# Projections: both rotary products on VectorE in a row, the low parts of queries and keys both on GpSimd

## What is computed

```python
q = (x @ Wq.T).reshape(B, T, 2 * H, hd)          # 16 half heads of 8
k = (x @ Wk.T).reshape(B, T, 2 * H, hd)
q = apply_rotary(rmsnorm(q), cos, sin)
k = apply_rotary(rmsnorm(k), cos, sin)
# apply_rotary: concatenate([x1 * c + x2 * s, -x1 * s + x2 * c])
```

## Time and profile before

| | us |
|---|---|
| median of 3 runs | 825.85 (824.96 to 826.49) |
| the profiled execution | 824.34 |
| its span in the profile | 822.6 |
| of it, from the first to the last sum L328 of the project phase | 23.25 to 108.83 |
| VectorE busy in the whole span | 589.5 |

### The profile page before, as it was taken

One profiled execution on the slowest core, in us unless ns is written; L12 is line 12 of the kernel. 1 busy time (PEld: TensorE's weight loads), 2 busy tenths in 40 slices (PEclk: granted clock), 3 DMA queues, 4 the chain that ended last, 5 costly groups with the idle time before them and its releaser, 6 DMA issues. The chain is left out here.

```text
span 822.6 us, 14081 instructions
## 1 busy us (share of the span) xinstructions
PE 629.0 (76%) x4241; PEld 324.2 (39%) x4242; DVE 589.5 (72%) x1424; ACT 480.6 (58%) x828; POOL 356.2 (43%) x506
## 2 busy tenths in 40 slices
PE   1366555999999999999999728877759877998920
PEld 1244332333333333333333216656536544654510
DVE  3899996779797979797977676797625443586734
ACT  2356665899999999999999512223324333444430
POOL 0234353234343434344433211117635777666653
PEclk9776865999999999999999956868759999999965
DMA  4200005940000000000000040012112222334241
GB/s 120 75 14 26 26 1 109 153 94 27 26 25 25 25 25 25 25 25 25 25 27 2 1 154 26 26 32 72 51 50 71 74 77 64 107 89 127 67 134 51
DMA packets 52978, 45.31 MB, mean 55 GB/s; under 512 B 5936, under 2 KB 47216, under 8 KB 52688
## 3 DMA queue, kind: packets, MB, share of 16 engines
q1 hardware_dynamic: 45600, 34.97, 16.5%
q0 software_dynamic: 4544, 9.35, 3.3%
q10 hardware_dynamic: 2800, 0.58, 0.3%
HBM read 15.72 MB, written 16.59 MB: 39 GB/s over the span
## 5 line engine op out<-in xcount | busy, mean ns | idle before, releaser
L733 ACT ACTIVATE attend_prob<-attend_ring 128x1024 f32<-128x1024 f32 (+1 forms) x320 | 280.0, 951 | 17.0 <-PE attend_ring L859 15.0
L682 POOL TENSOR_SCALAR_AFFINE_SELECT attend_prob<-attend_prob 128x256 f32<-128x256 f32 x256 | 117.2, 481 | 144.2 <-ACT attend_prob L733 143.9
L879 PE MATMUL attend_ps_o<-attend_prob,attend_v_slot 128*32 128x512 f32 (+3 forms) x1536 | 157.3, 498 | 0.0
L859 PE MATMUL attend_ring<-attend_qk_slot 32*128 32x512 f16 (+3 forms) x768 | 93.0, 334 | 15.5 <-ACT attend_prob L733 8.8
L1604 POOL DMA_INDIRECT expert_outputs<-expert_y_out,expert_goal_now x78 | 77.1, 988 | 53.1 <-POOL expert_goal_now L1599 20.3
L1790 PE MATMUL expert_ps_h<-w,expert_x_t 128*128 x156 | 89.9, 660 | 0.5 <-ACT expert_x_t L1724 0.5
L1737 ACT ACTIVATE expert_tanh<-expert_ps_h 128x256 f32<-128x256 f32 x78 | 30.0, 385 | 95.2 <-PE expert_ps_h L1790 95.2
L947 POOL DMA_INDIRECT slots<-rows,slot_index x64 | 61.5, 962 | 41.0 <-issue 41.0
L859 PEld LDWEIGHTS attend_ring<-attend_qk_slot 32*128 32x128 f16 x768 | 25.8, 91 | 130.5 <-ACT attend_prob L733 45.5
L1812 PE MATMUL expert_ps_y<-w,expert_hidden_t 128*128 x312 | 53.2, 294 | 14.4 <-DVE expert_y_out L1662 13.5
L1646 DVE SCALAR_TENSOR_TENSOR expert_silu<-expert_tanh,expert_ps_h 128x256 f32<-128x256 f32 x78 | 32.7, 419 | 42.6 <-ACT expert_tanh L1737 42.5
(11 more groups left out here) (235 smaller groups left out, 1223.0 us busy)
## 6 DMA issues: line engine op xcount, KB each, us to landing
attend_qk_slot<-qk_parts SPq DMA_DIRECT2D x16, 512.0 KB, 2.9
slots<-attend_zeros SPq DMA_DIRECT2D x26, 193.5 KB, 9.5
x_pairs<-slots SPq DMA_DIRECT2D x26, 193.5 KB, 2.6
expert_y_in<-expert_outputs SPq DMA_DIRECT2D x8, 512.0 KB, 4.8
xn_all<-project_xn SPq DMA_DIRECT2D x8, 256.0 KB, 2.3
w<-w_laid SPq DMA_DIRECT2D x1, 2048.0 KB, 7.7
rows<-rows SPq DMA_DIRECT2D x4, 512.0 KB, 3.6
out<-expert_result SPq DMA_DIRECT2D x8, 256.0 KB, 2.4
```

Source lines behind the costliest of these rows:

```text
L682: ins = nc.gpsimd.affine_select(out=edge, in_=edge, compare_op=ALU.is_ge, fill=0.0, base=0, pattern=[[0, 2], [1, P]], channel_multiplier=-1)
L733: nc.scalar.activation(probs(k, pair)[:, :, 0:width], scores[:, :, 0:width], ACT.Exp, scale=HD ** -0.5).then_inc(exp_made[u][pair], 1)
L859: ins = nc.tensor.matmul(dst[:, s * QC + at:s * QC + at + cols], qk_slot[slot][rows, T + j * P:T + (j + 1) * P], qk_slot[slot][rows, qc * ...
L879: ins = nc.tensor.matmul(ps_o[RB * s:RB * (s + 1), off:QC], v4[slot][:, j, s], probs(k, s // 2)[:, s % 2, at:at + cols], start=j == 0, sto ...
```

## The change

The sine product moves from GpSimd to VectorE, directly behind the cosine product. One semaphore, `turned`, takes the place of `cos_made` and `sin_made`. The low part of q moves from VectorE to GpSimd, ahead of the low part of k. Nothing is added or left out: each group still has two products and two low parts, of the same shapes.

```diff
--- before.py
+++ after.py
@@ -237,7 +237,7 @@
         squared = sem("squared")
         qkv_made, v_kept, half_normed = ([sem(f"{n}{h}") for h in range(2)] for n in ("qkv_made", "v_kept", "half_normed"))
         summed, rooted, rrms_made = (sem(n) for n in ("summed", "rooted", "rrms_made"))
-        cos_made, sin_made = sem("cos_made"), sem("sin_made")
+        turned = sem("turned")
         rotated, q_high, k_high, q_low, k_low = (sem(n) for n in ("rotated", "q_high", "k_high", "q_low", "k_low"))
         qk_turned = [sem(f"qk_turned{i}") for i in range(QUADS)]
         qk_kept = [sem(f"qk_kept{i}") for i in range(QUADS)]
@@ -282,7 +282,8 @@
 
                     g, odd = c
                     dve.wait_ge(half_normed[1], g + 1)
-                    nc.vector.tensor_tensor(halves(qcos), halves(qkn), rope(odd, 0), ALU.mult).then_inc(cos_made, 1)
+                    nc.vector.tensor_tensor(halves(qcos), halves(qkn), rope(odd, 0), ALU.mult)
+                    nc.vector.tensor_tensor(halves(qsin), halves(qkn), rope(odd, HD // 2), ALU.mult).then_inc(turned, 1)
                 if a:
 
                     g, odd = a
@@ -300,8 +301,7 @@
                     ins.then_inc(mom_made, 1)
                 if c:
                     g, odd = c
-                    dve.wait_ge(cos_made, g + 1)
-                    dve.wait_ge(sin_made, g + 1)
+                    dve.wait_ge(turned, g + 1)
                     once(dve, k_low, g)
                     cs = qcos.rearrange("p (t w h s d) -> p t w h s d", t=GT, w=2, s=2, d=HD // 2)
                     sn = qsin.rearrange("p (t w h s d) -> p t w h s d", t=GT, w=2, s=2, d=HD // 2)
@@ -337,12 +337,6 @@
                         ins = nc.vector.tensor_tensor(qkn.rearrange("p (t h d) -> p t h d", t=GT, d=HD)[:, tiles], qk_psum[:, tiles],
                                                       bcast(rrms.rearrange("p (t h) -> p t h", t=GT)[:, tiles], 3, HD), ALU.mult)
                         ins.then_inc(half_normed[h], 1)
-                if c:
-
-                    g, odd = c
-                    dve.wait_ge(q_high, g + 1)
-                    nc.vector.tensor_tensor(part[odd][0][:, :, 2:4], bcast(rot_h[0], 2, 2), part[odd][0][:, :, 0:2],
-                                            ALU.subtract).then_inc(q_low, 1)
 
             def after(u):
 
@@ -389,9 +383,9 @@
             def body(a, b, c, d):
                 if c:
                     g, odd = c
-                    pool.wait_ge(half_normed[1], g + 1)
-                    nc.gpsimd.tensor_tensor(halves(qsin), halves(qkn), rope(odd, HD // 2), ALU.mult).then_inc(sin_made, 1)
-
+                    pool.wait_ge(q_high, g + 1)
+                    nc.gpsimd.tensor_tensor(part[odd][0][:, :, 2:4], bcast(rot_h[0], 2, 2), part[odd][0][:, :, 0:2],
+                                            ALU.subtract).then_inc(q_low, 1)
                     pool.wait_ge(k_high, g + 1)
                     nc.gpsimd.tensor_tensor(part[odd][1][:, :, 1::2], bcast(rot_h[1], 2, 2), part[odd][1][:, :, 0::2],
                                             ALU.subtract).then_inc(k_low, 1)
```

## The result

The changed kernel took 812.91 us, the median of 4 runs (809.97 to 813.77); the kernel before 825.4 us (824.18 to 826.49). The ratio is 0.9842, with a 95% interval of 0.982 to 0.9864: 12.5 us faster (by 11.2 to 14.9). I had forecast 818.6 us, 7.2 faster, with 815.8 as the lower end. The direction is right, the size isn't. Two executions on record, 871.32 us of the kernel before and 1152.63 us of a delayed one, lie far above all others and enter no ratio.

What follows compares the result with a forecast made beforehand. VectorE was taken to bound the project phase, partly by waiting for GpSimd. First turn +0.6, five turns -7.4, group 6 to 7 0, end -0.4 gave -7.2 us: 825.85 becomes 818.6 us, range 815.8 to 822.0.

Steps and rivals of the forecast that it cites:

- Later phases are behind a barrier and just start earlier: After the project phase: the phases begin sooner, with no gain or loss of their own.
- What bounds the phase, and that 2.74 us of VectorE's turn is standing still: Project phase: VectorE bounds it, and waits 0.91 + 1.83 us per steady turn for GpSimd's SBUF reads.
- The price of the low part of q on GpSimd, 2.12 us: Project phase, GpSimd: the moved low part takes as long as L396, bounded by 1.90 and 2.88 us.
- Turns of 10.84 and 11.37 in alternation: Five turns, group 1's sum to group 6's: every other one waits for GpSimd; 62.56 becomes 55.1 us, -7.4.
- this chain can only get shorter: Steady turn: TensorE's chain, allowing the next sum at R + 10.75 (R: turn's start), would never run longer than counted.
- The first turn +0.6: Up to group 1's sum: the sine product adds 1.14 us, partly regained by L540; net +0.6 us.
- Group 6 to 7 unchanged: From group 6's sum to group 7's: TensorE's chain already bounds it, so 0, up to 0.5 us longer at lower clock.
- The tail -0.4: After the last sum: low parts alternate with quantization on GpSimd and VectorE, so 1.7 us of gain shrinks to 0.4.
- rival 2: Project phase: TensorE at upper clock, all turns 10.84 us, low parts in a row: 816.5 us, the most possible; chance 0.15.
- The base: Whole kernel before the change: median taken as 825.85 us, 1.5 above the profiled execution's 824.34.

Runs made afterwards that it cites:

- second profile: The changed kernel run again without any edit, against the kernel before: ratio 0.9854 (0.9833 to 0.9876).
- third profile: The changed kernel run once more without any edit, against the kernel before: ratio 0.988 (0.9861 to 0.9899).

## Why the prediction was wrong, point by point

The step that failed is "Later phases are behind a barrier and just start earlier"; the last point but one tells what the runs show in its place.

- *What bounds the phase, and that 2.74 us of VectorE's turn is standing still*: right. The other order of the low parts put the wait on the sine product, as worked out to 0.1 us. The Trainium skill (SBUF — State Buffer, section "Who interferes with whom") says that an instruction with two SBUF inputs on VectorE and one on GpSimd that reads SBUF exclude each other; the trace agrees, with 3.14 us for a product of 1.2.
- *The price of the low part of q on GpSimd, 2.12 us*: right, 2.12 in all eight groups of the first profile. The Trainium skill (GPSIMD Engine Reference, section "3.1 Elementwise — side-by-side cycle accounting") gives 1.96 times VectorE's time for a `tensor_tensor` add at N=2048 in fp32, which would have made it an estimated 2.39. For this operation and shape it is not borne out; the trace shows 2.12 to VectorE's 1.22, 1.74 times.
- *Turns of 10.84 and 11.37 in alternation*: half right. The wait behind the low part of q came in one turn of five, 11.24 us, and not in two. In the first of the five turns TensorE started its joint projection 3.41 us after the sum, where I had 5.30 for all; in the fourth the eight matmuls took 3.80 us, where I had 4.77 for all. The kernel before already had 3.63 to 5.49 us for them in its turns, so one turn was too narrow a base; "this chain can only get shorter" was wrong too, with 5.49 and 4.98 us in two turns of the changed kernel. In its second profile all five turns were 10.83 to 10.90. The five together gave 8.1 us in the first pair, for 7.4 forecast.
- *The first turn +0.6*: +0.54 (13.34 against 12.80). L534 of the changed kernel, L540 before, took 0.20 without GpSimd beside it, as counted.
- *Group 6 to 7 unchanged*: 10.94, 10.18 and 9.33 us in three profiles against 10.22 and 10.40; the joint projection in it took 4.98, 4.54 and 3.36 us against 4.26. TensorE's clock decides it, as said, with more scatter than the 0.5 us allowed.
- *The tail -0.4*: -0.84 in the first pair (24.74 to 23.90). The transposes started 19.4 us after the sum, as forecast. The third profile has 25.05, with the lower clock in the transposes: I had their length unchanged, and it isn't. By the mean of the three, 24.28, the -0.4 is hit by luck.
- Together, the phase gave 7.7 us in the first pair of profiles and 8.2 on the mean, for 7.2 forecast. That the attention phase started 7.0 us earlier, so near to 7.2, is luck: the 7.7 less the 0.72 by which the first sum was late. With 8.2 the total would be 817.2, inside the range.
- *"Later phases are behind a barrier and just start earlier"*: the failed step put what lies behind the barrier at nothing. In its place the profiles show 3.5 us (689.03 to 685.51): 0.84 in the attention phase, where the clock rose 12.4 and not 14.2 us in, 1.63 in the linear phase, where sixteen matmuls took 1.95 and not 3.62 us, and 1.05 in the expert phase, not traced to a piece. The instructions are the same. The other 1.9 us between the profiles' gain and that of the medians, 12.5, has no profile. The term belonged in the range, and mostly with one sign: over ten profiles in sessions of normal length, of eight variants of the kernel, the rest took 683.83 to 689.35 us, and the kernel before's 689.03 lies at the upper end, so some 5 us less were open and hardly anything more. That also refutes rival 2's "it can't be more". What would have warned me was the clock row of the page, which shows 0.5 to 0.8 of full speed through the linear phase, and the earlier trace rows, where the same eight matmuls took 2.82 or 4.77 us.
- *The base*: the median before came out as 825.4 for my 825.85, which is 0.45 us of the 5.7 missed.

What stays open is what picks the pattern. It is not the code alone (two profiles of the changed kernel had the rise at 12.4 us, the third at 16.4), nor the start time alone. Of 15 executions of the kernel before in the last session 9 lie within 1 us of their median of 824.7, and two 6 us below it (818.62 and 818.38). I did not show that the clock accounts for these. Their odds per kernel are not measured either; what is measured is that the changed kernel lies 10 to 13 us below the kernel before by the ratios, and that its project phase accounts for 8.2 of that. Whether the remaining 2 to 5 us belong to the change or to the draw of patterns is open.

## What to carry to other kernels

Before you price an instruction by its mean, look for its shortest row: where VectorE and GpSimd both read SBUF, part of the duration is the other engine's instruction, and the work that only moves in time costs 1.1 us, not 2.9. Put what excludes each other behind each other on one engine, and beside it what doesn't. And when a stage shrinks by a microsecond or two ahead of phases in which TensorE's clock comes and goes, look where your profile of before lies among several, and add their spread to the range (here 5.5 us of 825, nearly all of it below). Test with idle delays of different length and more than one profile of each; one delay, or one profile, can fall on the same pattern and mislead.

## What was not expected of the hardware

- The same sixteen matmuls of 128x128 took 3.62 or 1.95 us, with either kernel, in kernels that differ only in an idle delay of 1.7 us some 390 us earlier, profiled in different sessions. That the delay is the cause is not shown.
- The clock's rise in the attention phase lay 12.2 to 16.6 us after the start of the phase, and the phase took 339.5 to 340.9 us with it. The linear phase took 134.8, 138.3 or 140.0 us in sessions of normal length. At a rise of 12.2 to 12.4 us the attention phase took 339.5, at 14.1 to 14.7 it took 340.3 to 340.5, and at 16.4 to 16.6 it took 340.9.
- Waiting instructions alternate: whichever of VectorE and GpSimd had stood still got its turn next, also when the other's next instruction was already due (54.17 to 57.28 above, and the tail).
